# Attention and recurrence in one kernel: another dealing of steps and dense work, value products in two parts, key tiles in one room

## The reference, cut to what matters

```python
x = x + proj(softmax(mask(q @ k.T / sqrt(32))) @ v)       # q, k, v = split(x @ c_attn_w + c_attn_b)
def step(prev_h, xw_t):                                   # xw = x @ Wx + b
    next_h = jnp.tanh(prev_h @ Wh + xw_t)
    return (next_h, next_h)
_, hs = jax.lax.scan(step, h0, jnp.swapaxes(xw, 0, 1))
x = x + jnp.swapaxes(hs, 0, 1)
```

## Time and profile before

| what | us |
|---|---|
| median of 3 runs (lowest, highest) | 1730.66 (1730.48, 1731.11) |
| the profiled execution | 1726.08 |
| its span | 1724.3 |
| setup and first chunks | 0 to 75 |
| block 0 with trips 0 to 3 | 75 to 295 |
| blocks 1, 2 and 3 | 295 to 690, 690 to 1080, 1080 to 1480 |
| the last 128 steps | 1482 to 1724 |
| TensorE busy over the span | 1526.2 (89%) |
| VectorE, ScalarE, GpSimd busy | 821.8 (48%), 716.3 (42%), 383.1 (22%) |

### The profile page before, as it was taken

The page is one execution under the profiler, slowest core; times in us unless marked ns, Lnnn a source line. Parts: engine busy times, 40 slices in busy tenths (PEclk is TensorE's granted clock), DMA queues, the critical chain, the costliest instruction groups (busy, mean ns, idle before and its releaser), DMA issues.

```text
span 1724.3 us, 65681 instructions
## 1 busy us (share of the span) xinstructions
PE 1526.2 (89%) x28397; PEld 1291.9 (75%) x28397; DVE 821.8 (48%) x2596; ACT 716.3 (42%) x2285; POOL 383.1 (22%) x552
## 2 busy tenths in 40 slices
PE   5788888989999899999999999999999999777775
PEld 4677776878778777878788887888888888666664
DVE  5355454445444445545555555555555556222221
ACT  2345444434444344544444454544544446111111
POOL 0634342313122031312313131220311210000000
PEclk8888898999999999999999999999999999999999
DMA  7455445424434344535444455654555544000000
GB/s 250 167 155 172 134 154 167 122 79 137 119 102 128 85 145 126 152 113 149 131 120 137 110 154 148 161 155 113 148 140 137 139 127 103 8 15 9 15 9 14
DMA packets 135247, 204.72 MB, mean 119 GB/s; under 512 B 19880, under 2 KB 85672, under 8 KB 134448
## 3 DMA queue, kind: packets, MB, share of 16 engines
q1 hardware_dynamic: 107120, 125.50, 27.9%
q0 software_dynamic: 27840, 75.02, 12.9%
HBM read 133.06 MB, written 67.37 MB: 116 GB/s over the span
## 4 chain that ended last, share of the span: by engine, by line
PE 75%; DMA 7%; DVE 6%; issue 5%; ACT 5%; SPq 1%; POOL 1%; DVEq 0%; ACTq 0%; POOLq 0%
PE rec L915 23%; PE turned L851 8%; PE dense L421 7%; PE dense L422 6%; PE dense L423 6%; PE rec L908 6%; PE scores L843 4%; PE scores L915 4%; PE pv L864 3%; DVE pre L763 3%; DMA xin<-x 3%; DMA kq<-kq_dram 3%; ACT states L617 3%; PE pv L882 2%; DVE probs L712 1%
## 5 line engine op out<-in xcount | busy, mean ns | idle before, releaser
L915 PE MATMUL rec<-wh,states 128*32 128x128 f32 x14336 | 484.2, 276 | 67.3 <-ACT states L617 65.6
L915 PEld LDWEIGHTS rec<-wh,states 128*32 128x32 f32 x14336 | 375.4, 110 | 133.9 <-ACT states L617 101.3
L575 ACT ACTIVATE probs<-probs,nmax 128x128 f32<-128x128 f32 (+3 forms) x512 | 287.1, 561 | 194.7 <-DVE nmax L712 186.5
L617 ACT ACTIVATE states<-pre 128x32 f32<-128x32 f32 x512 | 133.2, 260 | 473.9 <-DVE pre L763 473.2
L712 DVE CUSTOM_DVE_ANT_0 probs<-scores,msk,nimg 128x128 f32<-128x128 f32 (+3 forms) x512 | 275.5, 545 | 58.0 <-PE scores L843 52.7
L763 DVE STREAM_TRANSPOSE pre<-rec 128x128 f32<-128x128 f32 x448 | 141.7, 316 | 334.6 <-PE rec L915 330.7
L851 PE MATMUL turned<-ident,probs 128*128 128x128 f32 x1280 | 240.8, 288 | 21.7 <-ACT probs L575 17.9
L843 PE MATMUL scores<-kq 96*128 96x128 f32 (+3 forms) x512 | 203.3, 402 | 19.7 <-DMA kq<-kq_dram 18.1
L851 PEld LDWEIGHTS turned<-ident,probs 128*128 128x128 f32 x1280 | 145.3, 141 | 79.5 <-issue 47.5
L516 POOL DMA_DIRECT2D kq_dram<-qs_hi x128 | 92.5, 725 | 319.7 <-DVE qs_lo L685 305.5
L721 DVE COPY probsT<-turned 128x128 f32<-128x128 f32 (+3 forms) x256 | 125.1, 489 | 67.6 <-PE turned L851 63.3
(11 more groups left out here) (153 smaller groups left out, 2246.0 us busy)
## 6 DMA issues: line engine op xcount, KB each, us to landing
kq<-kq_dram SPq DMA_DIRECT2D x96, 320.0 KB, 5.2
kq<-kq_dram SPq DMA_DIRECT2D x96, 256.0 KB, 4.5
kq<-kq_dram SPq DMA_DIRECT2D x96, 192.0 KB, 3.6
kq_dram<-qs_hi POOLq DMA_DIRECT2D x128, 128.0 KB, 2.7
kq_dram<-ks_hi POOLq DMA_DIRECT2D x128, 128.0 KB, 3.1
kq<-kq_dram SPq DMA_DIRECT2D x96, 128.0 KB, 2.9
xin<-x SPq DMA_DIRECT2D x32, 256.0 KB, 3.9
kq_dram<-qs_lo POOLq DMA_DIRECT2D x64, 128.0 KB, 3.4
```

The lines of the kernel that those rows point to most:

```text
L575: act.activation(probs[:, g % PROBS, 0:n], probs[:, g % PROBS, 0:n], ACT.Exp, scale=-1.0, bias=nmax[:, e, h:h + 1], accum_out=rowsum[:, e, ...
L617: act.activation(state_cells(g), pre[:].rearrange("p f (b z) -> p f b z", z=GROUP)[:, :, :, s], ACT.Tanh).then_inc(h_ready, 1)
L915: last = pe.matmul(rec_bank(g // GROUP)[Q * j:Q * j + Q, 0:P], state_tile(g - 1)[:, f, :], wh[:, f, P * j:P * j + P], start=False, stop=f ...
```

## The change

Four edits. The 128 steps of a block are laid by quarters: 32 steps evenly over the stretch between one projection's start (for the first quarter the end of the projection that completes the block) and the next. A value product is planned as two events, `vfirst` and `v`, of six matmuls each, with one bank. Dense work is dealt by weight: a head takes the first item of the list if its share of the weight that is left is over half of the item's weight; items of weight zero are taken at once. Key tiles are cut from one room of 5120 columns, of a size that goes with the block: five tiles in block 0, three in block 1, two in blocks 2 and 3; a load waits for the scores of the last group whose columns it overlaps.

```diff
+ROOM = 2 * HC * (P + S)
+def tile_places():
+    places, counts = [], [0] * (ROOM // (HC * 2 * P))
+    for group in range(GROUPS):
+        first = group // (8 * PAIRS) * 8 * PAIRS
+        size = HC * P * (block_of(group // 8) + 2)
+        n = (group - first) % (ROOM // size)
+        over = [m + 1 for m, (_, _, _, at, width) in enumerate(places)
+                if at < n * size + size and n * size < at + width]
+        counts[n] += 1
+        places.append((max(over, default=0), n, counts[n], n * size, size))
...
+    return places
...
     def values(g, e):
-        return [("v", g, e, 2.7), ("vstore", g, e, 0.0)]
+        return [("vfirst", g, e, 1.45), ("v", g, e, 1.45), ("vstore", g, e, 0.0)]
...
-            side, until = [], UNITS - 1
+            side, until = [], UNITS - 1 if g + 1 < TRIPS else H
...
-            if u % HC == HC - 1 and u // HC + TILES < GROUPS:
-                loads.append(("kqload", u // HC + TILES, 0, 0.0))
+            if u % HC == HC - 1:
+                loads += [("kqload", group, 0, 0.0) for group in range(GROUPS) if PLACES[group][0] == u // HC + 1]
...
-        take = len(side) if g >= TRIPS or h >= until else -(-len(side) // (until + 1 - h))
-        emit(side[:take])
-        side = side[take:]
+        share = sum(w for *_, w in side) / max(until + 1 - h, 1)
+        while side and (g >= TRIPS or h >= until or side[0][3] == 0.0 or share > side[0][3] / 2):
+            share -= side[0][3]
+            emit([side.pop(0)])
...
     for b in range(BLOCKS - 1):
-
-        first, last = ends[(b + 1) * PAIRS - 1] + 1, begins[(b + 2) * PAIRS - 1]
-        whole = sum(w for *_, w in main[first:last])
-        done, n = 0.0, 0
-        for at in range(first, last):
-            done += main[at][3]
-            while n < P and (done >= whole * (n + 0.5) / P
-                             or at + 1 == begins.get((b + 1) * PAIRS + n // STEPS)):
-                place.setdefault(at, []).append(b * P + n)
-                n += 1
-        assert n == P
+        first = ends[(b + 1) * PAIRS - 1] + 1
+        for n in range(PAIRS):
+
+            last = begins[(b + 1) * PAIRS + n]
+            whole = sum(w for *_, w in main[first:last])
+            done, t = 0.0, 0
+            for at in range(first, last):
+                done += main[at][3]
+                while t < STEPS and (done >= whole * (t + 0.5) / STEPS or at + 1 == last):
+                    place.setdefault(at, []).append(b * P + n * STEPS + t)
+                    t += 1
+            first = last
...
-                    if g >= TILES:
-                        sp.wait_ge(scores_ready, HC * (g - TILES + 1))
+                    after, n, *_ = PLACES[g]
+                    if after:
+                        sp.wait_ge(scores_ready, HC * after)
...
-                elif kind == "v":
+                elif kind in ("vfirst", "v"):
                     mine = slice(P * i, P * i + P)
-                    for f in range(C):
-                        last = split_product(d[:, :], xT_hi[:, f, mine], xT_lo[:, f, mine],
+                    for f in range(C // 2) if kind == "vfirst" else range(C // 2, C):
+                        last = split_product(bank("v", g, i)[:, :], xT_hi[:, f, mine], xT_lo[:, f, mine],
                                              wqkv_hi[:, f, 2 * D:3 * D], wqkv_lo[:, f, 2 * D:3 * D],
                                              f == 0, f == C - 1)
-                    last.then_inc(dense_ready, 1)
+                    if kind == "v":
+                        last.then_inc(dense_ready, 1)
```

More of the change, by code:

```diff
@@ L32 @@
 TURNED = 6
-TILES = 2
+ROOM = 2 * HC * (P + S)
 VTILES = 3
@@ L55 @@
 }
-DENSE_KINDS = ("q", "k", "v", "imgscore", "imgturn", "rowturn", "proj", "out")
+DENSE_KINDS = ("vfirst", "q", "k", "v", "imgscore", "imgturn", "rowturn", "proj", "out")
 def block_of(g):
     return g // PAIRS
+def tile_places():
[8 more added lines that the diff above has]
+        places.append((max(over, default=0), n, counts[n], n * size, size))
+    for n in range(len(counts)):
+        mine = [m for m, place in enumerate(places) if place[1] == n]
+        assert all(places[b][0] > a for a, b in zip(mine, mine[1:]))
+    return places
+PLACES = tile_places()
 def main_order():
-    out, seen, loads = [], set(), [("kqload", group, 0, 0.0) for group in range(TILES)]
+    out, seen, loads = [], set(), [("kqload", group, 0, 0.0) for group in range(GROUPS) if not PLACES[group][0]]
     loads += [("vload", group, 0, 0.0) for group in range(VTILES)]
@@ L201, in attention_recurrence @@
     for kind, g, i in ORDER["PE"]:
-        if kind in DENSE_KINDS:
+        if kind in DENSE_KINDS and kind != "v":
             n = turn % (2 if ("xsteps", 0, 0) in JOB else 3)
-            JOB[kind, g, i] = n, uses[n]
+            JOB["v" if kind == "vfirst" else kind, g, i] = n, uses[n]
             uses[n] += 1
             turn += 1
-            DONE[kind, g, i] = turn
+        if kind in DENSE_KINDS and kind != "vfirst":
+            DONE[kind, g, i] = len(DONE) + 1
         elif (kind, g) == ("xsteps", 0):
@@ L239, in attention_recurrence @@
         ks_lo = sb("ks_lo", [P, 2, 2 * P], F32R)
-        kq_tiles = sb("kq", [P, TILES, HC * (P + S)], F32R)
+        kq_tiles = sb("kq", [P, ROOM], F32R)
         vbuf = sb("vbuf", [P, 2 * D + VTILES * BLOCKS * P])
@@ L331, in attention_recurrence @@
         k_stored = [sem(f"k_stored{i}") for i in range(2)]
-        tile_loaded = [sem(f"tile_loaded{i}") for i in range(TILES)]
+        tile_loaded = [sem(f"tile_loaded{i}") for i in range(1 + max(place[1] for place in PLACES))]
         v_stored = [sem(f"v_stored{e}") for e in range(2)]
@@ L387, in heads_tile @@
         def heads_tile(group):
-            n = P + P * (block_of(group // 8) + 1)
-            return kq_tiles[:, group % TILES, 0:HC * n].rearrange("p (j n) -> p j n", j=HC)
+            _, _, _, at, size = PLACES[group]
+            return kq_tiles[:, at:at + size].rearrange("p (j n) -> p j n", j=HC)
         def rec_bank(k):
@@ L470, in _ @@
                                      kq_dram[part, r, :, c, e, 0:P + P * (p + 1)]
-                                     .rearrange("(j d) t -> d j t", d=Q)).then_inc(tile_loaded[g % TILES], 16)
+                                     .rearrange("(j d) t -> d j t", d=Q)).then_inc(tile_loaded[n], 16)
                 elif kind == "vload":
@@ L804, in _ @@
             for kind, g, i in ORDER["PE"]:
-                if kind in DENSE_KINDS:
-                    wait_bank(pe, kind, g, i)
+                if kind == "vfirst":
+                    wait_bank(pe, "v", g, i)
+                elif kind in DENSE_KINDS:
+                    if kind != "v":
+                        wait_bank(pe, kind, g, i)
                     d = bank(kind, g, i)
@@ L839, in _ @@
                     if j == 0:
-                        pe.wait_ge(tile_loaded[group % TILES], 48 * (group // TILES + 1))
+                        _, at, loads, *_ = PLACES[group]
+                        pe.wait_ge(tile_loaded[at], 48 * loads)
                     if g > 1:
```

## The result

The changed kernel took 1750.56 us (median of 4 runs, 1748.77 to 1758.75), the kernel before 1730.88 on the same chip: a ratio of 1.0107, 95% interval 1.0069 to 1.0145. It is slower by about 20 us, near the 1748 that was forecast.

What follows compares the result with a forecast made beforehand. TensorE's work bounds blocks 1 to 3; block 0 loses to idle time and lower clock. Terms -18 (a), +14 (e), -22 (b), +5 (c), +39 (d) sum to +18: 1744 us profiled, 1748 on the median's scale; range 1714 to 1769.

Steps and rivals of the forecast that it cites:

- (d): Last projection: casts of x stand ahead of a step's tanh, TensorE idles in eight trips, clock falls; +39 us together.
- six other loads: Loads of x with no step ahead: change little, +3 us.
- (e): Starts of blocks 1 to 3: first tile's load waits for the previous block's last scores; +14 us with clock drops.
- (a): Block 0 with five key tiles: 4.2 us of key waits, 7.8 of clock, 6 of small waits go; -18 us.
- Values in two parts: Value product split: no matmul added, bank held two heads longer, covered by the second bank; 0 us.
- (b): Blocks 1 to 3, steps spread evenly: of 36.9 us of waits between adjacent steps, 15 are left; -22 us.
- (c): Last stretch, from trip 15's projection to the end: 32 steps instead of 21, thinner cover, 0.15 us each; +5 us.
- the x load is short and the clock holds: Rival, chance 0.18: x lands in 2.6 us, gaps some 3.1 us, no clock drop; sum -13, 1718 us.
- The other order: Rival, chance 0.07: the step at the last projection does not stand behind the casts; sum -19, 1712 us.

Runs made afterwards that it cites:

- run 2: The changed kernel with key tiles as before, two places of 2560 columns used by turns: 1714.81 us.
- run 5: The changed kernel with the same tile sizes and counts, each block's first tile laid over columns that come free early: 1719.83 us.
- run 4: The kernel before with the dealing by weight and the values in two parts alone: 1719.28 us.
- runs 10 and 11: 10: run 7 with the value product as one event, 1724.37 us. 11: the kernel before with the dealing by weight alone, value product whole, 1753.31 us.
- run 7: The changed kernel with two key tiles as before and the casts of x held back: 1683.21 us.
- run 3: The kernel before with the even steps alone, each quarter's 32 steps spread over its own stretch: 1710.2 us.
- run 9: run 7 with the 128 steps of a block laid as before, by block and not by quarter: 1692.08 us.

## Why the prediction was right, and where its terms were not

**The casts behind the last projection, (d): right in mechanism and size.** Eight gaps of 31.3 us against 31.2 worked out, though in another order: in blocks 1, 2 and 3 they are 3.9, 3.7 and 4.4 us in the mean, for 4.15, 3.85 and 3.6. The landing of half an x was 3.3 us in the median, where I took 3.4 (tile xin, kernel after):

```profile
DMA to landing us min/median/max: 2.6/3.3/5.7
```

The fit in the Trainium skill, DMA: Bandwidth & Descriptors, section "Anatomy of one DMA — SWDGE (gpsimd) path", an estimate of 2.6 us for this transfer, agrees with the least landing again and not with the median. That section is on GpSimd's path, and x is loaded by SyncE. I priced the term at +39; holding the casts took 31.7 off the kernel after and 31.6 off run 2 (1714.8 to 1683.2). No run took the lower clock away by itself; by the granted clock it lasted 3.2 to 6.4 us behind each of the eight, and half of that is an estimate of some 19 us lost, where I had 16. Of the six other loads, +3, those in trips 1 to 4 changed little, as said: 17.2 us idle behind x, for 17.8 before. One sign did not come: ScalarE waited for x 51.0 us in 14 trips, 3.6 in the mean, and not over 4 in every one.

**Block boundaries, (e): right in sign, half the size.** I had 14.7 us of idle time, and 28.6 came. At block 1 the step that failed is "So the load of group 32 waits until all scores of block 0 are done, and its first score is next": the scores aren't the last thing the load waits for. In SyncE's order it stands behind group 34's load, which waits for the stores of the new trip's third chunk, and then nine issues share the queue. At blocks 2 and 3 the load did go out behind the scores; there "a load takes 4.5 us" failed, since the loads of two tiles go out at once and their median was 7.5 and 7.7. The tiles as a whole, here and in block 0, cost 36 (run 2), 31 of it by their place (run 5).

**Key tiles and block 0, (a): wrong.** "4.2 us go" failed: the old waits of trips 2 and 3 went, but waits of 2.8 to 4.9 us came at head 12 of each trip: the load that head 12 needs stands behind others let through early (in trip 2 group 19's behind group 21's). The fourth chunk, whose k is stored shortly before, is not enough to cause them: with two tiles (run 2) the longest wait at head 12 is 0.55 us, and the longest left is 3.72 at head 8 of trip 0. The clock that I had coming back in their place (7.8) did not come: over trips 0 to 3 it is 0.88, for 0.87 before. From trip 0's first score to TensorE's last work ahead of trip 4 it took 203.4 us before and 196.0 after, 7 less and not 18; with two tiles the whole block is shorter still (run 4). "The new dealing puts some on every second head", for which I took 6, is true only with the split (runs 10 and 11).

**Values in two parts: wrong.** "0, covered by the second bank" looked at the bank and not at the rule that deals the work. The split is worth 34 us (run 4 against 11) to 41 (run 7 against 10), the largest single gain of the change; without it the dealing costs 22.

**Steps, (b): right for the idle time.** The steps' waits in blocks 1 to 3 of the kernel after are some 13 us, for 15 predicted, without those that follow a load of x (the eight, 4.98 in trip 4, 2.71 and 2.44 in trips 8 and 12). Alone the even spread gains 21 (run 3), by my sum 22 less 5 at the end. But its worth hangs on the rest: 9 with the new dealing and held casts, and 4, not clear of noise, with the casts not held. There the even spread puts a step behind the casts in all eight trips: those gaps come to 30.4 us in run 2 and 23.9 in run 4. Counting pairs at 0.73 gave 12 for run 9's 9, but gives only 10 of run 3's 21, about what the waits lost; where the other 10 come from stays open.

**The last stretch, (c)**, was not tried by itself. From the projection in trip 15 to the last 128 steps, waits of steps come to 1.0 us in the trace after and none before, where I had +5.

**So the sum was right by cancelling.** It had +18 and the medians gave +20. The tiles came to +36, where (e) and the tiles' part of (a) make 14 - 4.2 - 7.8 = +2; the casts to +32, not +39; and with both taken out, dealing, split and steps gain 48 us (run 7), where my terms for them make -6 - 22 + 5 = -23. That these errors met within 2 us is luck. Of the rivals, "the x load is short and the clock holds" fell: the landing was the one I took, and the clock dropped behind gaps of 3.2 to 4.6 us. The other order did not occur.

## What to carry to other kernels

An item that a dealing rule counts as weightless still takes its place on an in-order engine: leave distance between a load and the instruction that waits for it, or give TensorE work meanwhile. Before trusting such a rule, work out at which head it takes its first item; one item too large for its share can empty the start of a trip. When one room is cut anew, put the next tile over the columns that come free first, and look at which loads stand ahead in the issuing queue, not only at the wait that the load itself states.

## What the runs showed of the hardware

More free tiles did not bring the tile that TensorE waited for earlier. With 21 issues instead of 12 in 24 us, single issues on SyncE's queue took up to 2.14 us against a median of 0.43, and the longest landing went from 3.6 to 5.9 us (run 2). At the start of block 2, with six issues of 256 KB at once, the median landing was 7.5 us, against 4.4 for this size over the whole execution. I had counted a landing as the same whatever else is under way.
